# Linear-attention layers: each fp32 projection product as three products of rounded fp32 parts

## What is computed

```python
xn = layernorm(x) * g + b                     # 4096 rows of 512
q  = softmax(heads(xn @ Wq + bq), axis=-1)    # over the columns of a head
k  = softmax(heads(xn @ Wk + bk + mask), axis=rows)
v  = (xn @ Wv + bv) * mask
y  = q @ (k.T @ v)                            # per head
out = x + silu(layernorm(y) * fa + fb) @ Wo + bo
```

## Time and profile before

| | |
|---|---|
| runs before, us | 5700.12, 5701.42, 5699.62 (median 5700.12) |
| the profiled execution, us | 5699.54 |
| its span, first to last instruction, us | 5697.7 |
| mean granted clock of TensorE | 0.976 of full |
| busy, share of span | PE 91%, DVE 73%, ACT 55%, POOL 58% |
| layer 2 in the span, us | 4478 to 5090 |
| layer 3 in the span, us | 5090 to 5698 |

### The profile page before, as it was taken

One profiled execution on the slowest core, in us unless ns is written; L12 is line 12 of the kernel. 1 busy time (PEld: TensorE's weight loads), 2 busy tenths in 40 slices (PEclk: granted clock), 3 DMA queues, 4 the chain that ended last, 5 costly groups with the idle time before them and its releaser, 6 DMA issues. The chain is left out here.

```text
span 5697.7 us, 58876 instructions
## 1 busy us (share of the span) xinstructions
PE 5175.6 (91%) x18688; PEld 2441.0 (43%) x18688; DVE 4163.2 (73%) x5558; ACT 3142.4 (55%) x5839; POOL 3289.4 (58%) x2200
## 2 busy tenths in 40 slices
PE   7888989888888969989999999999997899989998
PEld 2333333333333324434444444444443455444545
DVE  6999999999999983247777777777763455545454
ACT  4757566665757533327888888888872131312112
POOL 3879797888879761107898898898892000000000
PEclk9999999999999999988999999999998999999999
DMA  4021221212021205321111111111102302021101
GB/s 170 23 104 38 97 88 52 78 49 97 29 104 43 84 11 191 126 82 35 24 35 35 24 35 35 24 35 35 24 13 107 113 26 70 17 106 35 61 26 52
DMA packets 117511, 346.30 MB, mean 61 GB/s; under 512 B 13041, under 2 KB 14289, under 8 KB 102801
## 3 DMA queue, kind: packets, MB, share of 16 engines
q1 hardware_dynamic: 99280, 294.47, 15.8%
q0 software_dynamic: 9216, 33.56, 1.6%
q10 hardware_dynamic: 8704, 14.50, 0.7%
HBM read 274.29 MB, written 67.67 MB: 60 GB/s over the span
## 5 line engine op out<-in xcount | busy, mean ns | idle before, releaser
L425 POOL TENSOR_TENSOR mamba_hc<-mamba_h,mamba_bc 128x1024 f32<-128x1024 f32 x512 | 1218.2, 2379 | 360.7 <-DVE mamba_h L658 307.0
L805 PE MATMUL mamba_y<-mamba_hc,ident 128*128 128x512 f32 x2048 | 997.3, 610 | 272.1 <-POOL mamba_hc L425 269.8
L1282 POOL TENSOR_TENSOR attn_pair_sum<-attn_pair_sum,attn_prob 128x1024 f32<-128x1024 f32 x512 | 1204.2, 2386 | 56.0 <-ACT attn_prob L1397 56.0
L1441 DVE TENSOR_REDUCE attn_mx<-attn_ps_max 128x1 f32<-128x512 f32 x1536 | 966.9, 684 | 318.6 <-PE attn_ps_max L1305 313.7
L1397 ACT ACTIVATE attn_prob<-attn_ps_s 128x512 f32<-128x512 f32 x2048 | 1051.4, 602 | 78.3 <-PE attn_ps_s L1332 78.3
L528 ACT ACTIVATE mamba_da<-mamba_dt,mamba_a_neg 128x512 f32<-128x512 f32 x1024 | 691.1, 689 | 721.6 <-DVE mamba_h L658 718.0
L658 DVE TENSOR_TENSOR_SCAN mamba_h<-mamba_da,mamba_state,mamba_h 128x512 f32<-128x512 f32 x768 | 939.3, 1264 | 1.9 <-ACT mamba_da L528 1.9
L1332 PE MATMUL attn_ps_s<-attn_q_stack,attn_k_stack 100*128 100x512 f32 x2048 | 885.2, 436 | 5.2 <-ACT attn_prob L1397 5.2
L1305 PE MATMUL attn_ps_max<-attn_k_stack,attn_q_stack 98*128 98x512 f32 x2048 | 834.4, 412 | 33.4 <-ACT attn_own_exp L1406 16.6
L805 PEld LDWEIGHTS mamba_y<-mamba_hc,ident 128*128 128x128 f32 x2048 | 366.3, 191 | 856.0 <-POOL mamba_hc L425 458.2
L648 DVE TENSOR_TENSOR mamba_h<-mamba_du,mamba_bc 128x1024 f32<-128x1024 f32 x512 | 618.6, 1208 | 65.2 <-POOL mamba_state L427 56.8
(11 more groups left out here) (240 smaller groups left out, 6545.7 us busy)
## 6 DMA issues: line engine op xcount, KB each, us to landing
mamba_bc<-bc_dram SPq DMA_DIRECT2D x64, 1024.0 KB, 7.2
mamba_w<-in_in_proj_w_T SPq DMA_DIRECT2D x16, 2048.0 KB, 7.7
qk_parts<-qkv_pair POOLq DMA_DIRECT2D x64, 512.0 KB, 3.2
attn_k_stack<-qk_parts SPq DMA_DIRECT2D x96, 256.0 KB
attn_q_stack<-qk_parts SPq DMA_DIRECT2D x96, 256.0 KB
mamba_x_in<-in_x SPq DMA_DIRECT2D x16, 1024.0 KB, 5.5
mamba_w<-in_out_proj_w_T SPq DMA_DIRECT2D x8, 2048.0 KB, 8.4
lin_norm_x<-x_after_L SPq DMA_DIRECT2D x16, 1024.0 KB, 6.0
```

The source lines that it names most:

```text
L425: nc.gpsimd.tensor_tensor(hc[:, gs % HC_SLOTS, :, :], h[:, gs % H_SLOTS, :, :], bc[:, g, G:2 * G, :], ALU.mult).then_inc(s["hc_done"], 1)
L805: mm = nc.tensor.matmul(y[ct % 2][:, :], ident[:, :], hc[:, gs % HC_SLOTS, j, :], start=(g == 0 and j == 0), stop=(g == NG - 1 and j == G ...
L1282: nc.gpsimd.tensor_tensor(pair_sum[(hd * NGRP + g) % 2][:, at], first[:, at], prob[unit % SLOTS][:, at], ALU.add).then_inc(s["sum_done"], 1)
L1441: nc.vector.tensor_reduce(to, ps_max[seq % BANKS][:, :], AX.X, ALU.max, negate=own_block(i)).then_inc(s["bank_read"], 1)
```

## The change

Every factor of the four projections of a linear layer is split in two: a first part, which is the number rounded to the type `F32R` (a 4-byte type of rounded fp32), and a second part, which is the number less its first part, rounded to the same type. A product of two factors becomes three: first by first, first by second, second by first; second by second is left out. The products that accumulate are issued as `F32R`.

ACT makes the first part of the rows where it made `xn_t` before (`xn_first`), and then, with a second activation of the same bank, the full row, which is written over the `x` buffer from which it came (`in_x`). POOL subtracts the one from the other (`split_x`) into `xn_second`. For the weights ACT copies (`cut_w`) and POOL subtracts (`split_w`). For want of room, m1 and m2 share `xn_first` and `xn_second`, `q` serves as m2's `x`, `kn` as the residual buffer, and the raw weights land in parts of `v_all` and `k_t`; Wv and Wo share one place and are loaded again for each batch. Loads of `x` now wait for POOL's subtractions. K's first two column tiles take all products of the first part of the rows before those of the second, and so do three of the four output tiles. Q and V go over all four banks, and the start of the banks alternates from chunk to chunk (`bank`). Cut to its core:

```diff
-def norm_dve(nc, dve, m, own, it, src):
+def norm_dve(nc, dve, m, own, it, src, read=None):
-    dve.wait_ge(m.transposed, it * KD)
+    dve.wait_ge(*(read or (m.transposed, it * KD)))
...
+        xn_first = r.sb("xn_first", [P, KD, CH], F32R)
+        xn_second = r.sb("xn_second", [P, KD, CH], F32R)
+        m1 = Norm(r, keep, tb, xn=xn_first)
+        m2 = Norm(Room(nc, ctx, f"lin{layer}_out"), keep, tb, x=q, xn=xn_first)
+        w_first = [r.sb(f"w_{n}_first", [P, KD, D], F32R) for n in ("q", "k", "v")]
+        w_second = [r.sb(f"w_{n}_second", [P, KD, D], F32R) for n in ("q", "k", "v")]
-        x_res = r.sb("x_res", [P, TT, D])
+        x_res = kn
...
+        def bank(it, i):
+            return mb[(2 * (it % 2) + i) % 4]
+        def x_banks(it):
+            return [bank(it, k) for k in range(KD)] if it else tb
+        def w_raw(i, n):
+            if n == 1:
+                return v_all[:, (i + 1) * KD:(i + 2) * KD, :]
+            return k_t[:, :, D:2 * D] if n % 2 == 0 else k_t[:, :, 2 * D:3 * D]
+        def in_x(m, k):
+            return m.x[:, :, k * P:(k + 1) * P]
...
+            def load_x(it):
+                sp.wait_ge(s["second_1"], it * KD)
+                norm_load(sp, m1, src, it)
...
+                sp.wait_ge(s["k_turned"], b * QT + 2 * CH // P)
+                load_w(sp, W_VO, 2 * b + 2, "Wo")
+                sp.wait_ge(s["kv_mm"], (b + 1) * QT)
...
+            def split_w(i, n):
+                pool.wait_ge(w_cut[i], n)
+                nc.gpsimd.tensor_tensor(w_second[i][:, :, :], w_raw(i, n), w_first[i][:, :, :].bitcast(F32),
+                                        ALU.subtract).then_inc(w_split[i], 1)
+            def split_x(m, full, second, it):
+                for k in range(KD):
+                    pool.wait_ge(m.turned, it * KD + k + 1)
+                    pool.wait_ge(s[full], it * KD + k + 1)
+                    nc.gpsimd.tensor_tensor(by_tile(xn_second[:, k, :]), in_x(m, k), by_tile(xn_first[:, k, :].bitcast(F32)),
+                                            ALU.subtract).then_inc(s[second], 1)
...
+                norm_pool(nc, pool, m2, b * NC_B)
+                split_w(W_VO, 2 * b + 2)
+                for c in range(NC_B):
+                    it = b * NC_B + c
+                    split_x(m2, "full_2", "second_2", it)
+                    if c + 1 < NC_B:
+                        norm_pool(nc, pool, m2, it + 1)
...
+                    for mt in range(2):
+                        pe.wait_ge(m1.turned, it * KD + mt + 1)
+                        pe.wait_ge(s["full_1"], it * KD + mt + 1)
+                        k_products(it, mt, ((0, 0), (1, 0)), True, False)
+                    for mt in range(2):
+                        k_products(it, mt, ((0, 1),), False, True).then_inc(s["k_mm"], 1)
+                    for mt in range(2, KD):
+                        pe.wait_ge(s["k_done"], it * KD + mt - 1)
+                        k_products(it, mt, ((0, 0), (1, 0), (0, 1)), True, True).then_inc(s["k_mm"], 1)
...
+                                for i, j in ((0, 0), (0, 1), (1, 0)):
+                                    mm = nc.tensor.matmul(bank(it, 2 + t)[:, :], (xn_second if i else xn_first)[:, k, at],
+                                                          (w_second if j else w_first)[which][:, k, :],
...
                     if more:
+                        pe.wait_ge(s["full_1"], (it + 1) * KD)
+                        norm_pe(nc, pe, m1, it + 1, x_banks(it + 1), lambda k: (s["v_biased"], it * TT + k + 1))
...
+                    for t in range(TT - 1):
+                        pe.wait_ge(m2.turned, it * KD + t + 1)
+                        pe.wait_ge(s["full_2"], it * KD + t + 1)
+                        o_products(t, ((0, 0), (0, 1)), True, False)
+                    for t in range(TT - 1):
+                        o_products(t, ((1, 0),), False, True).then_inc(s["o_mm"], 1)
+                    pe.wait_ge(s["full_2"], (it + 1) * KD)
+                    o_products(TT - 1, ((0, 0), (0, 1), (1, 0)), True, True).then_inc(s["o_mm"], 1)
...
                 def norm(it):
                     act.wait_ge(s["v_mm"], it * TT)
+                    act.wait_ge(s["o_mm"], it // NC_B * NC_B * TT)
+                    norm_act(nc, act, m1, it, ACT.Identity, lambda k: g[:, k:k + 1], lambda k: bvec[:, k:k + 1], x_banks(it))
+                    for k in range(KD):
+                        nc.scalar.activation(in_x(m1, k), by_tile(x_banks(it)[k][:, :]), ACT.Identity, scale=g[:, k:k + 1],
+                                             bias=bvec[:, k:k + 1]).then_inc(s["full_1"], 1)
...
-                    norm_dve(nc, dve, m2, own2, it, lambda t: y_banks(c)[t][:, :])
+                    norm_dve(nc, dve, m2, own2, it, lambda t: y_banks(c)[t][:, :], (s["second_2"], it * KD))
```

More of the change, by code:

```diff
@@ L1622, in stage_linear @@
         v_all = r.sb("v_all", [P, QT, D])
-        q = r.sb("q", [P, TT, D])
+        W_Q, W_K, W_VO = range(3)
         q_red = r.sb("q_red", [P, TT * heads])
@@ new lines, in k_products @@
+                def k_products(it, mt, parts, first, last):
+                    for k in range(KD):
+                        cols_of = slice(mt * P, (mt + 1) * P)
+                        for i, j in parts:
+                            if mt == 0:
+                                pe.wait_ge(*((s["second_1"], it * KD + k + 1) if j else (m1.turned, it * KD + k + 1)))
+                            weights = (w_second if i else w_first)[W_K][:, k, cols_of]
+                            rows_t = (xn_second if j else xn_first)[:, k, :]
+                            mm = nc.tensor.matmul(bank(it, mt % 2)[:, :], weights, rows_t, start=first and k == 0 and (i, j) == parts[0],
+                                                  stop=last and k == KD - 1 and (i, j) == parts[-1])
+                    return mm
@@ L1788, in _, with o_products @@
                     elif b + 1 < NB:
[L1789 to L1791 removed]
+                        norm_pe(nc, pe, m1, it + 1, x_banks(it + 1), lambda k: (s["out_done"], it * TT - TT + k + 1))
+                    pe.wait_ge(w_split[W_VO], 2 * b + 2)
+                    def o_products(t, parts, first, last):
                         for k in range(KD):
[L1793 to L1795 removed]
+                            for i, j in parts:
+                                if t == 0:
+                                    pe.wait_ge(*((s["second_2"], it * KD + k + 1) if i else (m2.turned, it * KD + k + 1)))
+                                mm = nc.tensor.matmul(y_banks(c)[t][:, :], (xn_second if i else xn_first)[:, k, t * P:(t + 1) * P],
+                                                      (w_second if j else w_first)[W_VO][:, k, :],
+                                                      start=first and k == 0 and (i, j) == parts[0],
+                                                      stop=last and k == KD - 1 and (i, j) == parts[-1])
+                        return mm
+                    for t in range(TT - 1):
[6 more added lines that the diff above has]
+                    o_products(TT - 1, ((0, 0), (0, 1), (1, 0)), True, True).then_inc(s["o_mm"], 1)
         @block.scalar
@@ L1838, in _ @@
                     norm(0)
+                    cut_w(W_Q, 1)
+                    cut_w(W_VO, 1)
                     act.wait_ge(s["mask_set"], 1)
@@ L1850, in _ @@
                     act.wait_ge(s["o_mm"], it * TT)
+                    act.wait_ge(s["v_mm"], (b + 1) * NC_B * TT)
                     norm_act(nc, act, m2, it, ACT.Silu, lambda k: batch_film[:, 0, k:k + 1], lambda k: batch_film[:, 1, k:k + 1],
                              y_banks(c))
+                    for k in range(KD):
+                        nc.scalar.activation(in_x(m2, k), by_tile(y_banks(c)[k][:, :]), ACT.Silu, scale=batch_film[:, 0, k:k + 1],
+                                             bias=batch_film[:, 1, k:k + 1]).then_inc(s["full_2"], 1)
                 if b + 1 < NB:
                     norm((b + 1) * NC_B)
+                    cut_w(W_VO, 2 * b + 3)
         @block.vector
```

101 lines of the change are left out of this document (56 added, 45 removed).

## The result

The changed kernel takes 5624.9 us in the median of four runs (5622.9 to 5627.1), the kernel before 5700.8 us on the same chip: a ratio of 0.9867 with a 95% interval of 0.985 to 0.9884. It is faster by 75.9 us; 84 us were forecast.

A forecast was written before the change was run, and what follows sets the result against it. TensorE bounded both halves before; VectorE and ScalarE would then set the first half's steady chunk. Gains of 39.3 us (layer 2) and 44.3 us (layer 3), together 84 us of 5699.5 us, gave 5616 us; range 5575 to 5668.

The forecast's parts named there:

- The products: All four projections: each fp32 product becomes three rounded ones of 0.233 us, a projection 11.2 us for 13.75 us.
- The rival of half an fp32 instruction: Projections: rounded products take 0.215 us, 38 us more gain, 5578 us; chance 0.12.
- that of no gain: Projections: a rounded product over 128 rows takes 0.430 us, a projection 6.9 us longer, above 6000 us; chance 0.03.
- The new work: Each chunk, in each half: four more ScalarE activations, 0.66 to 0.77 us apart, and four GpSimd subtractions of 1.31 us.
- The rival of a dear subtraction: GpSimd's subtractions before K and in the second half: at 2.38 us each the kernel slows to 5721 us; chance 0.08.
- Its break-even: GpSimd's subtractions in both halves: from 2.21 us per subtraction on, the kernel is slower than before.
- The steady chunk: First half: VectorE and ScalarE set the time after Q's last tile; 41.6 us a chunk, 4.0 us less, K 12.2 us.
- The second half: TensorE sets it: 16.5 us a chunk for 19.05, 9.5 us gained per batch, 19 us per layer.
- the term between the batches: From one batch's output to the next K: 3.65 us of TensorE standing plus low clock, -4.5 us per layer.
- the 1.3 us for the table load of the second batch: Second batch's first chunk, first half: the exponential's table load is no longer covered, 1.3 us lost per layer.
- the last chunks: Last chunk of each first half: gains of 3.8 and 2.8 us in layer 2, 5.8 and 4.8 us in layer 3.
- the rival of the low clock: Chunk ends, first half: low clock returns, 1.7 us in 12 chunks, about 5636 us, or 5658 with K's first pass; chance 0.18.

The follow-up runs named there:

- ScalarE's order: Changed kernel with ScalarE making both forms of the first two rows before copying the last two V tiles, then of the last two rows: 5585.4 us.
- the run with two passes: Changed kernel with, in the last chunk before the second batch, output products reading rounded rows issued ahead of those reading the second part: 5616.1 us.
- The filling: Changed kernel with unread products of weights with weights in TensorE's waits at the chunks' ends: 5615.9 us.

## Why the prediction was right, point by point

**The products** at 0.233 us hold for 128 rows and for every projection: Q in the chain is 11.21 us, 11.2 forecast. The rival of half an fp32 instruction (0.215) and that of no gain (0.430 at the full clock) fall: three products are 0.70 us for 0.86. Counting one pass for each against the four passes of true fp32 that the Trainium skill names ("FP8 and Floating Point Precision", TensorE Precision Notes) gives 0.645 us for the three, an estimate; the trace has 0.70, and the measurement decides.

**The new work:** GpSimd's 1.31 us was 1.29; rounded output costs it nothing that shows. The rival of a dear subtraction holds as a mechanism: doubled in the first half alone it made the kernel 25.6 us slower than before. Its break-even lies lower than worked out, since a doubling in the first half cost 101.5 us where its sum gives 83, part of it at the low clock after the waits inside K.

**The steady chunk:** the shift of the bound to VectorE and ScalarE was right; V removed changed nothing, and ScalarE's order alone gave 2.7 us a chunk. 41.6 us were forecast, 41.8 measured. That K came out at 12.23 us for 12.2 is luck: GpSimd takes 0.57 us of it, not 1.0, and without GpSimd it is 11.65 us, not 11.2.

**The second half** had TensorE as its limit, 16.5 us a chunk as forecast. Between the batches TensorE stood 3.8 us for 3.65, and the run with two passes shows that the shared rounded rows were the reason. The K behind it takes 14.2 us in layer 2 and 13.2 in layer 3, and 12.3 in both with two passes: 1.9 and 0.9 us, of which the prediction had put some 0.85 each into the term between the batches. In the row of the steady chunks they are in part made up by a cost that did not arise: the 1.3 us for the table load of the second batch. ScalarE loads the table early and is done with it 26 us before the exponential (layer 2, in order of time):

```profile
4779.44 1.28 ACT L1934 ACT_TABLE_LOAD   x1
...
4807.08 1.92 ACT L1934 ACTIVATE lin_q<-lin_q 128x2048 f32<-128x2048 f32 x1 [26.36 <-DVE lin_q L2031]
```


**The mis-sized term** is the last chunks, 10.2 us for 17.2. Up to the first turning of k layer 3 came as forecast: 27.6 and 27.5 us from K's end, for 27.5. What is missing lies in K, where three of the four take 13.2 us, and behind that point, where the prediction had no term: from the first turning of k to the first applying of q 24.2 to 24.4 us, for 22.6 and 22.8 before, 6.6 us in all. It had put the low clock into this place as 1 us in layer 2 and as nothing in layer 3. What spoke against it, one stretch with 3.8 us of standing in 8.1 and a PEclk of 1.00, was taken as a rule; the new stretches, with waits of 1.3, 1.9 and in layer 2 4.5 us, read 0.86 to 0.94. So the rival of the low clock came true in part, at other places than its sum assumed: of the twelve K's that follow another chunk of their batch, nine take 12.1 to 12.3 us and three 13.2, slow from their second microsecond on; a clock below 1.00 at K's begin was one of the prediction's signs of being wrong. In this execution all three are in last chunks; in other runs they are elsewhere. The filling shows that the clock is the reason in the turnings; for K the PEclk (0.87) is a reading, not a test.

**Layer 2's second halves** fell 4.1 us short, 14.9 for 19, but not for a reason of layer 2. Where nothing is added, a second batch's half takes 77.9 us for 87.4, 9.5 less, as forecast. In this execution layer 2 has 1.4 us more, in each batch, in the first turning and the second applying of q, behind 7.3 us of standing that was there before the change too, and in the second batch 1.55 us more in its last output products; in other runs, with the same instructions there, layer 2 has none of it (first line: the changed kernel; second: the run with two passes; layer 2's second batch):

```profile
4987.16 4.92 PE L1860 MATMUL lin_turn_bank<-lin_kv,lin_q_t 128*128 128x128 f32 x32
4977.49 3.74 PE L1864 MATMUL lin_turn_bank<-lin_kv,lin_q_t 128*128 128x128 f32 x32
```

So the total is in part chance: of layer 3's 20.2 us for 19, 1.2 come from the kernel before, whose profiled execution had such a slow applying (4.95 us for 3.74) in layer 3's first batch.

## What to carry to other kernels

When the bound engine's work shrinks by a fifth, follow the chain of the engines that it covered before summing its gain: here VectorE and ScalarE took the bound at 4 of 7.7 us per chunk, and in this half the next gain came from ScalarE's order, 37.4 us, while leaving out two thirds of V brought nothing that shows. Copies that a matrix product waits for should alternate with those that nobody waits for yet, so that the first rows are ready in both forms early. And a shorter TensorE block leaves waits, which can cost a second time through the clock: size them, and fill or remove the ones just ahead of work on the path.

## What was not expected of the hardware

In the last chunk's K above TensorE does not restart slowly after its wait: it runs at the 2.4 GHz pitch for its first microsecond and only then falls to 0.43 us per product. And the same wait does not always cost the same. In the run with ScalarE's new order, TensorE stands 1.3 and 1.95 us around the turning of q in layer 3's first last chunk, 1.2 and 1.95 us in its second; the stretches from there to the applying of q:

```profile
5209.50:5237.80 28.30, 25.12 (x209) 24.70 (x209) 7.82 (x14) 10.05 (x17) 0.00 (x0) 0.94 0.11 39
5473.70:5500.50 26.80, 23.64 (x209) 23.09 (x209) 7.78 (x14) 10.05 (x17) 0.00 (x0) 1.00 0.12 41
```

The last output products of a layer follow 2.52 us of standing for ScalarE each time; in one execution of the changed kernel they took 12.95 us in layer 2 and 11.41 us in layer 3, and in the run with filling products 12.95 us in layer 3. Stretches of layer 3's last output products, of the changed kernel and then of the run with filling:

```profile
5604.20:5620.00 15.80, 13.28 (x65) 10.64 (x63) 6.25 (x10) 5.46 (x8) 5.04 (x4) 1.00 0.40 149
```

```profile
5592.00:5612.70 20.70, 12.97 (x49) 10.11 (x48) 5.75 (x9) 4.29 (x7) 4.99 (x4) 0.90 0.35 125
```

Over the changed kernel and the runs that keep the output's three products, a second batch's half takes either 77.9 to 78.4 us (11 times) or 80.5 to 81.0 us (13 times). In the long ones both the second applying of q (4.6 to 5.0 us for 3.7 to 3.9) and the last output products (12.95 us for 11.4) are slow, in the short ones neither: the two, some 50 us apart, go together. Sums over single executions therefore move by a few microseconds at places that an edit leaves alone. What decides between the two is not settled by these runs.
